# Folding the closing unit's narrow diagonal block into its wide one on VectorE, so that TensorE's row sums read one block less

## What is computed

```
q = rope(x @ Wq); k = rope(x @ Wk); v = x @ Wv
att = einsum('bhgqd,bhkd->bhgqk', q, k) / sqrt(32)
att = where(causal, att, -inf)
probs = softmax(att)
ctx = einsum('bhgqk,bhkd->bhgqd', probs, v)
out = ctx @ Wo
```

## Time and profile before

| | us |
|---|---|
| three runs, median (lowest to highest) | 1485.77 (1485.64 to 1491.04) |
| the profiled execution, its own time | 1488.36 |
| its span, first to last instruction | 1486.7 |
| TensorE busy in the span | 1462.1 |
| VectorE busy | 982.9 |
| GpSimd busy | 695.1 |
| ScalarE busy | 582.9 |

### The profile page before, as it was taken

How to read it: one execution, slowest core, us unless ns; L and a number is a source line. 1 busy time by engine, 2 the same in 40 slices (tenths; PEclk the granted TensorE clock), 3 DMA queues, 4 the chain that set the end, 5 groups by cost and what they waited for, 6 DMA issues and landing times. The chain is left out here.

```text
span 1486.7 us, 25706 instructions
## 1 busy us (share of the span) xinstructions
PE 1462.1 (98%) x9000; PEld 1165.2 (78%) x9000; DVE 982.9 (66%) x2753; ACT 582.9 (39%) x1058; POOL 695.1 (47%) x384
## 2 busy tenths in 40 slices
PE   7999999999999999999999999999999999999999
PEld 7999999888888875555555555555489999999988
DVE  6756674647474848898998888889555444444533
ACT  4333333212111136666666666666632211221220
POOL 1322222633343438999999999999602101010101
PEclk9999999999999999999999999999999999999999
DMA  6555554342325271443333444430262423232311
GB/s 244 188 186 193 194 204 163 133 128 99 114 87 149 95 177 41 109 91 80 80 80 80 97 101 105 95 80 23 58 249 71 141 72 118 96 121 92 114 70 71
DMA packets 138164, 174.32 MB, mean 117 GB/s; under 512 B 43056, under 2 KB 93104, under 8 KB 137776
## 3 DMA queue, kind: packets, MB, share of 16 engines
q1 hardware_dynamic: 109744, 149.69, 33.9%
q10 hardware_dynamic: 28304, 23.14, 4.8%
HBM read 109.88 MB, written 67.67 MB: 119 GB/s over the span
## 5 line engine op out<-in xcount | busy, mean ns | idle before, releaser
L1785 ACT ACTIVATE at_probs<-ps 128x512 f32<-128x512 f32 (+1 forms) x640 | 314.9, 560 | 166.8 <-PE ps L1694 162.0
L71 DVE CUSTOM_DVE_ANT_0 ps<-ps,at_score_mask 128x512 f32<-128x512 f32 (+1 forms) x480 | 270.7, 623 | 26.1 <-PE ps L1683 24.2
L401 POOL TENSOR_TENSOR f_x_ring<-f_x_ring,f_half_bias 128x1024 f32<-128x1024 f32 x32 | 76.6, 2395 | 404.1 <-DVE f_low_s L745 404.1
L1626 POOL TENSOR_TENSOR at_added<-at_added,at_probs 128x2048 f32<-128x2048 f32 (+1 forms) x60 | 210.3, 3506 | 2.7 <-ACT at_probs L1785 0.7
L1711 PE MATMUL ps<-at_probs,at_vs 128*32 128x512 f32 (+3 forms) x1536 | 151.0, 496 | 0.3 <-POOL at_probs L1605 0.3
L77 PE MATMUL f_ps<-f_wt_hi,f_hT_hi 128*128 128x400 f32 (+1 forms) x384 | 132.2, 344 | 3.3 <-DVE f_hT_lo L718 3.3
L78 PE MATMUL f_ps<-f_wt_lo,f_hT_hi 128*128 128x400 f32 (+1 forms) x384 | 130.6, 340 | 0.0
L79 PE MATMUL f_ps<-f_wt_hi,f_hT_lo 128*128 128x400 f32 (+1 forms) x384 | 130.6, 340 | 0.0
L77 PE MATMUL ps<-f_wt_hi,f_hT_hi 128*128 128x400 f32 (+1 forms) x384 | 130.2, 339 | 0.0
L78 PE MATMUL ps<-f_wt_lo,f_hT_hi 128*128 128x400 f32 (+1 forms) x384 | 130.1, 339 | 0.0
L79 PE MATMUL ps<-f_wt_hi,f_hT_lo 128*128 128x400 f32 (+1 forms) x384 | 130.0, 339 | 0.0
(11 more groups left out here) (213 smaller groups left out, 3513.5 us busy)
## 6 DMA issues: line engine op xcount, KB each, us to landing
f_x_ring<-in_L_attn_resid SPq DMA_DIRECT2D x16, 512.0 KB, 3.5
x<-f_x_ring SPq DMA_DIRECT2D x16, 512.0 KB, 3.3
early<-x SPq DMA_DIRECT2D x16, 512.0 KB, 3.8
scr_q_hi<-qkv_rope_hi ACTq DMA_DIRECT2D x32, 256.0 KB, 2.0
scr_q_lo<-qkv_rope_lo ACTq DMA_DIRECT2D x32, 256.0 KB, 2.3
scr_ctx<-at_ctxn SPq DMA_DIRECT2D x32, 256.0 KB, 2.7
shared<-scr_ctx SPq DMA_DIRECT2D x16, 512.0 KB, 5.0
f_x_ring<-x SPq DMA_DIRECT2D x16, 512.0 KB, 5.6
```

Source lines behind the costliest of these rows:

```text
L71: return dve.tensor_tensor_reduce(out=src[:, 0:keys], in0=src[:, 0:keys], in1=mask, scale=1.0, scalar=part_max[:, g, own] if c else -3.0e3 ...
L401: pool.tensor_tensor(x_ring[:, u, :], x_ring[:, u, :], half_bias[:], ALU.add).then_inc(bias_added, 1)
L1626: pool.tensor_tensor(added[:, heads, :], first, probs[:, (NU * n + u) % PROBS, heads, :], ALU.add).then_inc(added_done, 1)
L1785: act.activation(probs[:, (NU * n + u) % PROBS, g, cols], score_ps[x % BANKS][:, cols], ACT.Exp, scale=SCALE).then_inc(exp_done, 1)
```

## The change

In every group but the last, VectorE adds the narrow block of unit 9 onto the last 128 columns of its wide block, in place in `probs`, once the unit's products are finished. It does so after the third row maximum of the closing unit. TensorE's second `sums` of the group then reads unit 9's wide block alone, after a wait on the new semaphore `folded`. The last group is left as it was.

```diff
+        folded = sem("folded")
...
+        FOLD_AT = 3
...
+                fold = half and n < NG - 1
                 for u in APART[half]:
-                    for j, at, cols in blocks(u):
+                    if fold and u == NU - 1:
+                        pe.wait_ge(folded, n + 1)
+                    parts = blocks(u)[:1] if fold else blocks(u)
+                    for j, at, cols in parts:
                         for g in range(G):
                             last = pe.matmul(out[g * DH:(g + 1) * DH, at], ones[:], probs[:, (NU * n + u) % PROBS, g, cols],
-                                             start=u == 0, stop=u in LAST and j == units[u][1][-1])
+                                             start=u == 0, stop=u in LAST and j == parts[-1][0])
                 last.then_inc(slot_filled, 1)
...
+            def fold(n):
+
+                (_, _, wide), (_, _, narrow) = blocks(NU - 1)
+                tile = probs[:, (NU * n + NU - 1) % PROBS, :, :]
+                into = tile[:, :, wide.stop - P:wide.stop]
+                dve.wait_ge(unit_done, NU * n + 2 * NU)
+                dve.tensor_tensor(into, into, tile[:, :, narrow], ALU.add).then_inc(folded, 1)
...
-                    for m, it in placed[n, u]:
+                    for at, (m, it) in enumerate(placed[n, u]):
+                        if n < NG - 1 and u == NU - 1 and at == min(FOLD_AT, len(placed[n, u]) - 1):
+                            fold(n)
                         slot_item(m, it)
```

## The result

The changed kernel takes 1564.39 us (median of four runs, 1559.55 to 1569.91) against 1488.40 for the kernel before in the runs beside it: a ratio of 1.0502, with a 95% interval of 1.0479 to 1.0525. It is slower by about 76 us, where 2.8 us less had been forecast.

The account below looks back on a forecast made before the run. TensorE was taken to bound the attention stage. Saving 3.3 us, or 2.5 if one closing loses 0.54, was taken as 2.8: 1485.8 - 2.8 = 1483.0 us, range 1480.5 to 1488.5.

Parts of the forecast that it names:

- The bound and the removed work: In the attention stage TensorE sets the pace; 128 columns fewer at each of 15 closings save 0.22 us each, 3.3 us.
- What the addition takes: On VectorE at a closing, the addition waits for GpSimd's mask and ends 0.55 us after it, at 651.71.
- the pair of the earlier trace: Mask from 1071.35 to 1072.45 on GpSimd, then VectorE's subtraction ahead of GpSimd's product; taken to show VectorE gets in between.
- The lead of 0.16 us: At a closing, VectorE can ask at 650.98, ahead of GpSimd's product at 651.14; losing this lead would let the product first.
- The rival on the other side: At all fifteen closings GpSimd's product gets in first and the next scores come 0.83 us late: 12.5 us, 1498; chance 0.08.
- The tenth closing: The one closing where the addition was expected to wait for GpSimd's product, until 883.46, with 0.54 us lost.
- The covers: Other work or idle time around a closing that hides the addition, its delay of VectorE and GpSimd's delay, costed at nothing.
- the four reads of `added` and unit 8: TensorE work ahead of the wide block's weight load at 651.92, said to leave the addition 0.2 us early.
- the idle time ahead of the transposition: VectorE's 1.42 us idle behind the turn in a closing, said to swallow the addition with 0.4 us left.
- What would show it wrong: Signs: an addition of 1.9 us or more in most closings, TensorE's weight loads waiting for it, or groups as long as before.

Follow-up runs that it names:

- the run in which GpSimd pauses: Changed kernel, with GpSimd's product by the reciprocals in a closing made to wait for VectorE's addition: 1483.38 us against 1488.65 for the kernel before.
- the pause ahead of the mask: Changed kernel, with a closing's first mask on GpSimd made to wait until ScalarE has copied the turn: 1490.78 us.
- The run where nobody waits: Changed kernel, with the addition writing a tile nobody reads and TensorE summing the narrow block as before, without waiting for the addition: 1535.64 us.
- the run where TensorE waits: Kernel before, without the addition, with TensorE waiting ahead of unit 9's sums in fifteen groups for GpSimd's last instruction of the closing: 1562.75 us.

## Why the prediction was wrong

*The bound and the removed work* were right. TensorE bounds the stage, and 128 columns cost 0.22 us a closing: the run in which GpSimd pauses gives back 3.4 us from closing to closing where the text had 3.3. That its median of 1483.4 stands where 1483.0 had been put for the change itself is in part luck: the median is 5.3 us below that of the kernel before beside it, the two profiled executions are 2.7 apart, and the rows don't show where the median gains more than that.

*The step that failed* is "What the addition takes", in its last sentence: "So the addition, asked for at 650.98 inside a mask that ends at 651.16, should end 0.55 later, at 651.71." It rests on the pair of the earlier trace rows, in which VectorE got in between mask and product. That row shows a difference that the text passed over: the mask there came after 0.86 us of idle time of GpSimd, and the mask of a closing comes straight behind an add. One pair was taken for the rule; it isn't the only one in the trace, as the text had it, but the two in the projection stage lie early in GpSimd's run as well. In the closings of all these runs, VectorE got in only where the instruction that ran on GpSimd had begun after a pause, or where the next was free to go only after VectorE had asked; with neither, it waited for the end of the run every time, which in the changed kernel made 3.9 us of 0.73. The lead of 0.16 us, on which the text weighed its chances, decided nothing: in the closing shown the addition asks 0.21 us before the product starts, and goes last.

The text on the pause ahead of the mask says that in the two places where VectorE got in the first instruction came after a pause. For the subtraction at 277.74 that isn't so: the pause was one instruction further back.

*The rival on the other side* was right that the product goes ahead, and wrong in the reason and the size. Its reason was a lead that VectorE loses, and VectorE kept the lead. Its size was one product; what goes ahead is the rest of the run, product, mask and subtraction, 3.1 us. With the run cut to one product the loss was 8.9 us where it had 12.5. The tenth closing, priced at 0.54, was the same error: it counted to the end of one instruction.

*The covers* were counted against 0.7 us and failed at 3.9. Of the two that failed, the four reads of `added` and unit 8 keep TensorE busy until 655.45 + 0.85 = 656.30, 1.46 us after the addition has asked, so 2.5 are left; and the idle time ahead of the transposition covers 1.4 of VectorE's delay, so the slots come late too. The run where nobody waits shows the second by itself, 47 us, and the run where TensorE waits shows what the first can cost, 73; the two don't add to the 76, since TensorE waits once for both.

*The clock* stands in no step. The text read that it was full, and priced every wait at its length. In the changed kernel the waits and what is late with them are 37 of 71 us, and the other 34 come with the lower clock. The kernel before has no idle stretch of TensorE over 0.3 us in these groups, but for one of 0.51 ahead of the last closing, with the clock at 1.00, so nothing in its rows gave that price.

What would show it wrong was named rightly: an addition over 1.9 us in most closings, and a wait of TensorE's weight loads for it.

## What to carry to other kernels

Before VectorE gets an instruction with two inputs in SBUF, look at what GpSimd does from then on. If GpSimd has been running without a pause, count to the end of its run, not of the instruction that is running: VectorE may get in earlier, but in these closings it never did. If the instruction must stand there, make GpSimd wait for it: a pause of 0.6 us on an engine with 2.5 us to spare turned 5% slower into 0.45% faster. And a wait of about 2 us on a TensorE that was never idle is priced by the clock as well as by its length.

## What was not expected of the hardware

- GpSimd's run kept VectorE out for 3.9 us, across three changes of instruction, while the same instructions of GpSimd lasted no longer than alone (1.26, 0.67 and 1.25 us). A pause of 0.2 us before the instruction that was running let VectorE in behind it. Why a pause matters, and what GpSimd holds across a run, stays open: the runs show when it happens and not the mechanism. Two things a rule on pauses alone doesn't cover: a product whose semaphore came 0.06 us after VectorE asked gave way without any pause, and at 278.42 and 291.00 in the kernel before VectorE got in between two instructions of a short run.
- After idle stretches of TensorE of 2.5 us the granted clock fell in 10 cases of 14 (to 0.84 or 0.91 over the groups shown). After ones of 1.9 us it fell in 11 of 14 where TensorE waits for GpSimd, but in 7 of 13 where it waits for a slot; after ones of 0.62 or 0.85 it stayed full, but for the one fall behind the last 0.62. The first of the two runs with 1.9 us lost 73 us, 28 of them as idle time, and the second 47. Why the same length costs so differently isn't shown.
